# One store of all codes, loads let go as others land, and the second half's lookup regrouped, in a recommendation tower

## The reference

```python
e = jnp.stack([tbl_0[ids[:, 0]], ..., tbl_15[ids[:, 15]]], axis=1)          # (2048, 16, 16)
A = jnp.repeat(r_x0, 16, axis=1)                                            # (2048, 624, 16)
Bm = jnp.repeat(e, 39, axis=2).reshape(2048, 624, 16)
z = jnp.einsum('bnh,bnd,nk,khd,kd->bkh', A, Bm, alpha, w, hv[..., 0])
h = jnp.concatenate([z.reshape(2048, 256), dense_ctx], axis=1)
h = jnp.maximum(h @ W_top1 + b_top1, 0.0)
h = jnp.maximum(h @ W_top2 + b_top2, 0.0)
y = h @ W_top3
```

## Time and profile before

| what | value |
|---|---|
| runs | 177.66, 178.49, 180.9 us; median 178.49 us |
| profiled execution | 178.92 us, of which the profile's span is 177.0 us |
| PE busy in the span | 164.0 us (93%) |
| DVE busy | 142.5 us (80%) |
| POOL busy | 110.9 us (63%) |
| ACT busy | 66.0 us (37%) |

### The profile page before, as it was taken

The page is one execution under the profiler, slowest core; times in us unless marked ns, Lnnn a source line. Parts: engine busy times, 40 slices in busy tenths (PEclk is TensorE's granted clock), DMA queues, the critical chain, the costliest instruction groups (busy, mean ns, idle before and its releaser), DMA issues.

```text
span 177.0 us, 5041 instructions
## 1 busy us (share of the span) xinstructions
PE 164.0 (93%) x2131; PEld 124.3 (70%) x2131; DVE 142.5 (80%) x177; ACT 66.0 (37%) x176; POOL 110.9 (63%) x116
## 2 busy tenths in 40 slices
PE   6549898968997999999999999999999999999993
PEld 1338696736984879696969696969686967776671
DVE  2978797893799999999899979996999899495000
ACT  3440788084881125212431243123403341451141
POOL 2777777777747777777777777777777776000000
PEclk9999999996999999999999999999999999999999
DMA  5889999999999997989498948694559360000000
GB/s 87 307 120 327 246 275 161 270 373 264 283 334 250 345 320 150 363 248 230 79 352 240 216 160 300 189 230 104 183 219 222 48 231 6 2 4 0 0 4 0
DMA packets 15085, 34.26 MB, mean 194 GB/s; under 512 B 6618, under 2 KB 10582, under 8 KB 11990
## 3 DMA queue, kind: packets, MB, share of 16 engines
q1 hardware_dynamic: 10162, 31.51, 58.9%
q0 software_dynamic: 3584, 0.92, 6.6%
q10 hardware_dynamic: 1316, 1.50, 2.9%
HBM read 33.88 MB, written 0.04 MB: 192 GB/s over the span
## 4 chain that ended last, share of the span: by engine, by line
PE 69%; DMA 13%; DVE 4%; ACT 3%; SPq 3%; issue 3%; POOL 3%; DVEq 0%
PE bank L927 17%; PE bank L842 17%; PE bank L848 15%; PE bank L894 11%; DMA ids_half_dram<-ids_half 6%; PE bank L915 5%; PE bank L835 4%; DMA ids_b<-ids_half_dram 3%; POOL e L478 3%; DMA e<-tbl_dram,ids_all 3%; DVE prod L642 2%; SPq L446 2%; DMA ids_all<-ids_dram 1%; ACT apart L724 1%; PE bank L856 1%
## 5 line engine op out<-in xcount | busy, mean ns | idle before, releaser
L478 POOL DMA_INDIRECT e<-tbl_dram,ids_all x112 | 110.7, 988 | 38.7 <-issue 33.2
L642 DVE TENSOR_TENSOR prod<-x,bank 128x2048 f32<-128x2048 f32 x40 | 90.3, 2279 | 8.8 <-issue 4.6
L927 PE MATMUL bank<-prod,m_w 128*32 128x256 f32 x640 | 38.6, 382 | 2.5 <-DVE prod L642 2.5
L894 PE MATMUL bank<-table,onehot 125*128 125x64 bf16 (+1 forms) x288 | 31.9, 198 | 2.3 <-DVE low L537 2.3
L842 PE MATMUL bank<-tower,w_z 128*128 128x256 f32 x128 | 32.8, 403 | 0.7 <-ACT tower L743 0.7
L894 PE MATMUL bank<-low,onehot 125*128 125x64 bf16 (+1 forms) x288 | 31.8, 197 | 0.0
L894 PE MATMUL bank<-rest,onehot 125*128 125x64 bf16 (+1 forms) x288 | 31.8, 199 | 0.0
L894 PEld LDWEIGHTS bank<-table,onehot 125*128 125x128 bf16 x288 | 27.4, 98 | 5.7 <-issue 2.9
L927 PEld LDWEIGHTS bank<-prod,m_w 128*32 128x32 f32 x640 | 19.1, 109 | 17.0 <-issue 3.5
L848 PE MATMUL bank<-tower,w 128*128 128x256 f32 x128 | 30.7, 382 | 0.1
L842 PEld LDWEIGHTS bank<-tower,w_z 128*128 128x128 f32 x128 | 24.2, 199 | 6.3 <-ACT tower L743 3.1
(11 more groups left out here) (60 smaller groups left out, 85.4 us busy)
## 6 DMA issues: line engine op xcount, KB each, us to landing
x<-x_dram SPq DMA_DIRECT2D x16, 1024.0 KB, 8.1
x<-x_dram SPq DMA_DIRECT2D x16, 512.0 KB, 12.4
ids_b<-ids_half_dram SPq DMA_DIRECT2D x7, 576.0 KB
e<-tbl_dram,ids_all POOLq DMA_INDIRECT x112, 4.7
prod<-windows_c_dram ACTq DMA_DIRECT2D x1, 768.0 KB
prod<-windows_c_dram ACTq DMA_DIRECT2D x1, 512.0 KB, 5.6
w_z<-w_z_dram SPq DMA_DIRECT2D x1, 512.0 KB
w<-w_dram SPq DMA_DIRECT2D x1, 512.0 KB, 11.0
```

The source lines that it names most:

```text
L478: nc.gpsimd.indirect_dma_start(out=e[:, tile, f * D:(f + 1) * D], out_offset=None, in_=t[f"tbl_{f}"][:, :], in_offset=bass.IndirectOffsetO ...
L642: nc.vector.tensor_tensor(prod[:, s % NPROD, :].rearrange("p (q b) -> p q b", q=HP), x0[:, tile % NX, :].rearrange("p (q b) -> p q b", q=H ...
L894: made = nc.tensor.matmul(o_bank[i % 2][:, at:at + m * D], onehot[:, n % 2, g, HOT.index(f), tile * P:(tile + 1) * P], parts[part][:, KT_A ...
L927: made = nc.tensor.matmul(z_bank[q * ZW:(q + 1) * ZW, a * HB:(a + 1) * HB], m_w[:, UNIT_OF[g], hp * ZW:(hp + 1) * ZW], prod[:, s % NPROD, ...
```

## The change

- **The store.** Before, the codes of half 1 (9 rows) are stored first, and those of halves 2 to 7 in six more stores, after the loads of tiles 1 and 2. Now one store takes all 72 rows in the place of the first.
- **The loads.** Before, SPq issues all early loads without waiting for one another, except that half 2's codes wait for the six stores. Now seven waits stand among them: each such load is issued when a certain earlier load has landed. Their order is another one too.
- **Half 1's fields.** The nine fields of half 1 are divided among its three fills in another way, so that its first window piece needs two fills instead of three.
- **Half 2's planes and picks.** Plane 0 of half 2 moves on DVE from step 4 to step 2, ahead of `multiply(3)`. Its first two fills (7 and 8) move on PE from step 5 to step 4, between the contractions of steps 3 and 4; the third (9) from step 6 to step 5.
- **The windows.** On PE, `turn_windows(0, 2)` moves ahead of pick 5, `turn_windows(1, 0)` ahead of half 0's `l1`, `turn_windows(1, 1)` right behind its first part. On ACT, `spread_e(1, 0)` moves ahead of `keep_z(0)`, `spread_e(1, 1)` ahead of the emptying of `l1`, and half 3's plane 1 (line 731) one step later. On DVE the masks of fills 5 and 6 move ahead of `multiply(4)`.

```diff
+SECOND_FILLS = [[[1, 2], [4]], [[5, 12], [15]], [[7, 10, 13]]]
...
-PLANE_STEPS = {1: [0, 0], 2: [4, 4], 3: [5, 6], ...
-PICK_STEPS = {1: [BEFORE, 2, 3], 2: [5, 5, 6], 3: [9, 10, 11], ...
+PLANE_STEPS = {1: [0, 0], 2: [2, 2], 3: [5, 6], ...
+PICK_STEPS = {1: [BEFORE, 2, 3], 2: [4, 4, 5], 3: [9, 10, 11], ...
...
-    return 2 * p + 2 if n == 0 else FIRST_FILLS[n + 1]
+    return 2 * FILL_PACK[j] + 2 if n == 0 else FIRST_FILLS[1] + 2 if (n, j) == (1, 0) else FIRST_FILLS[n + 1]
...
-            sp.dma_start(ids_rows[1], ids_half[1:IDS:NH, :]).then_inc(ids_stored[0], 16)
+            sp.dma_start(ids_rows.rearrange("n f b -> f n b"), ids_half[:]).then_inc(ids_stored, 16)
...
             load_x0(1)
             load_x0(2)
-            for n in range(2, NH):
-                sp.dma_start(ids_rows[n], ids_half[n:IDS:NH, :]).then_inc(ids_stored[1], 16)
+            sp.wait_ge(in_x0[1], 16 * x0_loads(1))
+            load_ids(2)
             sp.dma_start(b_w3[:], t["b_w3"]).then_inc(in_b_w3, 16)
+            sp.wait_ge(in_x0[2], 16 * x0_loads(2))
+            load_x0(3)
+            sp.wait_ge(in_ids_b[2], 16)
             load_ctx()
             sp.dma_start(w1_z[:], ...).then_inc(in_w1, 16)
-            sp.wait_ge(ids_stored[1], 16 * (NH - 2))
-            load_ids(2)
-            load_x0(3)
+            sp.wait_ge(in_x0[3], 16 * x0_loads(3))
+            load_x0(4)
+            sp.wait_ge(in_w1, 16)
             load_ids(3)
+            sp.wait_ge(in_x0[4], 16 * x0_loads(4))
             sp.dma_start(w2[:], ...).then_inc(in_w2, 16)
-            load_x0(4)
...
                 if s == 4:
+                    spread_e(1, 0)
                     keep_z(0)
-                    spread_e(1, 0)
+                    spread_e(1, 1)
                     act.wait_ge(in_b_w3, 16)
...
                 if s == 5:
                     find_apart(3)
+                elif s == 6:
                     make_plane(3)
...
                 if s == 2:
                     for unit in CONTRACTS[2]:
                         contract(unit)
+                    turn_windows(0, 2)
                     for i in PICKS[2]:
                         pick_rows(i)
                 if s == 4:
-                    for unit in CONTRACTS[4]:
-                        contract(unit)
+                    contract(CONTRACTS[4][0])
+                    for i in PICKS[4]:
+                        pick_rows(i)
+                    contract(CONTRACTS[4][1])
+                    turn_windows(1, 0)
                     pe.wait_ge(in_ctx, 16 * N_CTX_LOADS)
                     pe.wait_ge(in_w1, 16)
                     for job in JOBS[4]:
                         fill_t(job)
+                    turn_windows(1, 1)
```

More of the change, by code:

```diff
@@ L69 @@
 HALF_FILLS = [[[4, 7, 10, 13]], [[15], [1, 2]], [[5, 12]]]
-FILLS = [(_n, _runs) for _n in range(8) for _runs in (FRONT_FILLS if _n == 0 else HALF_FILLS)]
+SECOND_FILLS = [[[1, 2], [4]], [[5, 12], [15]], [[7, 10, 13]]]
+FILLS = [(_n, _runs) for _n in range(8) for _runs in (FRONT_FILLS if _n == 0 else SECOND_FILLS if _n == 1 else HALF_FILLS)]
 FIRST_FILLS = {_n: 0 if _n == 0 else len(FRONT_FILLS) + (_n - 1) * len(HALF_FILLS) for _n in range(9)}
@@ L146 @@
 BEFORE = -1
-PLANE_STEPS = {1: [0, 0], 2: [4, 4], 3: [5, 6], **{n: [UH * (n - 1) - 4, UH * (n - 1) - 3] for n in range(4, NH)}}
-PICK_STEPS = {1: [BEFORE, 2, 3], 2: [5, 5, 6], 3: [9, 10, 11], **{n: [UH * (n - 1) - 2, UH * (n - 1) - 1, UH * (n - 1)] for n in range(4, NH)}}
+PLANE_STEPS = {1: [0, 0], 2: [2, 2], 3: [5, 6], **{n: [UH * (n - 1) - 4, UH * (n - 1) - 3] for n in range(4, NH)}}
+PICK_STEPS = {1: [BEFORE, 2, 3], 2: [4, 4, 5], 3: [9, 10, 11], **{n: [UH * (n - 1) - 2, UH * (n - 1) - 1, UH * (n - 1)] for n in range(4, NH)}}
 KEEP_STEPS = {1: [1, 4, 4], 2: [5, 6, 7], 3: [9, 10, 11], **{n: [UH * (n - 1) - 1, UH * (n - 1), UH * (n - 1) + 1] for n in range(4, NH)}}
@@ L170, in act_planes_by, with kept_at @@
     return sum(of <= n for of in ACT_HALVES)
-def kept_at(n, p):
-    return 2 * p + 2 if n == 0 else FIRST_FILLS[n + 1]
+def kept_at(n, j):
+    return 2 * FILL_PACK[j] + 2 if n == 0 else FIRST_FILLS[1] + 2 if (n, j) == (1, 0) else FIRST_FILLS[n + 1]
 PE_IDS = 1
@@ L307, in program @@
         in_small = sem("in_small")
-        ids_stored = [sem(f"ids_stored_{n}") for n in range(2)]
+        ids_stored = sem("ids_stored")
         in_ids_b = {n: sem(f"in_ids_b_{n}") for n in range(PE_IDS, NH)}
@@ L439, in _ @@
             load_x0(0)
-            sp.wait_ge(ids_stored[0], 16)
+            sp.wait_ge(ids_stored, 16)
             load_ids(1)
@@ L652, in _ @@
                     sum_rows(3)
-                for i in KEEPS.get(s, []):
+                for i in KEEPS[4] if s == 3 else KEEPS.get(s, []) if s != 4 else []:
                     mask_rows(i)
-                if s != 4:
-                    for plane in PLANES.get(s, []):
-                        make_plane(*plane)
+                for plane in PLANES.get(s, []):
+                    make_plane(*plane)
                 for i in KEEPS.get(s, []):
@@ L660, in _ @@
                 if s == 4:
-                    for plane in PLANES[4]:
-                        make_plane(*plane)
                     dve.wait_ge(in_b_w3, 16)
@@ L692, in spread_e @@
             def spread_e(n, j):
-                act.wait_ge(rows_kept, kept_at(n, FILL_PACK[j]))
+                act.wait_ge(rows_kept, kept_at(n, j))
                 for i in range(j + 1):
@@ L802, in _ @@
                     make_plane(2)
-                if g in (0, 1) and s > 0:
+                if g in (0, 1) and s not in (0, UH):
                     spread_e(n, g + 1)
@@ L998, in _ @@
                         fill_t(job)
-                if s == 1 or g == 2:
+                    turn_windows(1, 1)
+                if s == 1 or g == 2 and n > 0:
                     turn_windows(n, g)
-                elif g == 4 and n + 1 < NH:
+                elif g == 4 and 0 < n < NH - 1:
                     turn_windows(n + 1, 0)
-                fills = PICKS.get(s, []) if s > 2 else []
+                fills = PICKS.get(s, []) if s > 2 and s != 4 else []
                 units = CONTRACTS.get(s, []) if s not in (0, 2, 4) else []
@@ L1017, in _ @@
                         pick_rows(i)
[L1018 to L1022, removed]
+                if s in (UH, 2 * UH):
                     for i in fills:
```

## The result

The changed kernel was slower, by a little: 181.3 us against 179.69 for the kernel before in four runs each, ratio 1.0161 [1.0093, 1.0229]; a later set of 12 runs gave 180.33 us and 1.0069 [1.0022, 1.0115]. The second, of more runs, is the better measure. The forecast was 177.0 us with a range up to 179.6: wrong in sign. The profiled execution took 180.15 us, its span 178.3 (before 178.92 and 177.0), so the trace shows 1.3 us to be explained.

What follows compares the result with a forecast made beforehand. PE was taken to bound the kernel from step 7's contraction on, so only the start-up counted: 178.92 us profiled less 1.5 is 177.4, and runs' median 0.43 lower gives 177.0 us, range 175.0 to 179.6.

Steps and rivals of the forecast that it cites:

- 33.5 taken: Start-up: half 2's codes, behind tile 2 only, land at 33.5 us instead of 36.2, ends 32.3 and 34.5.
- 42.6 taken: Start-up: `multiply(5)` starts 9.1 us after half 2's codes land, at 42.6 us instead of 45.32, 2.7 us gained.
- The rule that step 7's contraction follows half 3's plane by 7.74 us: End of start-up: the 7.74 us from half 3's plane on DVE to step 7's contraction on PE stay as before.
- the turning point of 48.1 us: Half 3's codes: from a landing at 48.1 us on, each microsecond later is one lost.
- DVE's 8.1 us: DVE from half 2's codes: plane, two multiplications, two masks and a sum end by 33.5 + 8.1 = 41.6 us.
- Half 3's codes: 46.6 us: Start-up loads: half 3's codes land at 46.6 us, ends 44.3 and 49.8, so step 7 gains 1.5 us.
- The second rival: Start-up loads: waits leave gaps, half 3's codes land at 49.8 us, 1.7 us lost, 180.2 us; chance 0.17.
- The stores' removal returns something between nothing and the 2 us: Thin stretch of 28 to 30 us: without the six stores, half 3's codes come 1.0 us sooner.
- 40.7 us for `w_z`: Start-up loads: `w_z` lands 5.9 us or more ahead of half 3's codes, about 40.7 us; wanted at 43.
- The waits for landings cost something: Loads of tile 3, tile 4 and half 3's codes: gaps cost nothing to 3.5 us, 1.3 taken.
- The third rival: Start-up: nothing gained, `w` lands at 51.4 instead of 49.6 or the one store delays half 1's codes; 178.5 us, chance 0.13.
- What it gains there the whole gains: From step 7's contraction (55.87 us) on PE is unaltered, so its gain there is the whole kernel's gain.

Runs made afterwards that it cites:

- e1: Kernel before with one store of all codes in place of the first, without the six later stores: 179.85 us, 0.9997.
- e9: e8 with the four dense-context loads issued right behind half 2's codes instead of behind their landing: 176.74 us, 0.9872.
- e3: Changed kernel without its six waits for landings, order of the loads kept: 181.73 us, 1.0144 against the kernel before.
- e10: e8 without its five waits for landings: 181.38 us, 1.0063 against the kernel before.
- e8: Changed kernel with the dense context in whole rows, and half 3's codes and `w` ahead of tile 4: 178.0 us, 0.992 against the kernel before.
- e4: Changed kernel with half 3's plane 0 one step later on DVE, behind `multiply(6)`: 179.59 us, 1.0012 against the kernel before.
- e7: Changed kernel with half 3's codes and `w` loaded ahead of tile 4: 179.13 us, 0.9959 against the kernel before.
- e2: Changed orders on PE, DVE and ACT, with the stores and loads of the kernel before: 180.81 us, 1.0037.
- e6: Kernel before with the dense context in memory as whole rows: 179.41 us, 1.0033.
- e13: e8 with the second copy of the dense context in partitions 64 to 79 instead of 32 to 47: 176.65 us, 0.9849.
- after: The changed kernel itself, in its first profiled execution: 180.15 us.
- e11: e9 with `w_z` and `w` also laid out in whole rows of 4 KB: 177.87 us, 0.9929 against the kernel before.
- e5: Changed kernel with the dense context in memory as whole rows: 179.99 us, 0.9943 against the kernel before.
- e14: e9 with the second copy of the dense context in partitions 64 to 79: 177.29 us beside 179.44, too few runs for an interval.

## Why the prediction was wrong

**What held.** Half 2's codes landed at 30.7 us (33.5 taken; the lower end was 32.3), since tile 2, ahead of them, had landed at 29.2 us where 31.8 was counted with; whether it was the stores or the dense context's loads that had held it up no run shows. `multiply(5)` began at 41.26 us, 42.6 taken, and picks 7 and 8 stand between the contractions of steps 3 and 4. The rule that step 7's contraction follows half 3's plane by 7.74 us held at 7.77 and, in the 12 runs' profile, 7.75; so did the turning point of 48.1 us: 48.70 gives 0.6 of loss, 49.78 gives 1.66. The one store cost nothing to be seen: half 1's codes reached ACT at 21.3 us (22.6 before), and `multiply(2)`, behind half 1's fills, began at 30.00 us (30.77 before). `l1`'s clock fell as feared (0.88 in 40 to 45 us and 0.73 in 44 to 50, after PE had stood 1.84 us), and `l2` behind it waited for `w` anyway. (Two sums of the prediction are a little off without effect: the pieces of DVE's 8.1 us come to 7.7, and half of 3 × 2.29 is 3.4.)

**The step that failed** is "Half 3's codes: 46.6 us". They landed at 48.7 and 49.8 us in the two profiles. The second rival, "the steps starve the DMA engines", came true with its turning point and, at 180.2 us, nearly its price. In the first profile the price was met partly by luck: only 0.6 of the 1.3 us come by this step, the rest by PE's stand at 79 us. Two terms were mis-sized.

- *"The stores' removal returns something between nothing and the 2 us"; 1.0 was taken.* The runs show no return. e1's time can't tell 1.0 us (0.6%) from nothing, but in its trace the thin stretch is there without any of the six stores. I had read 87 GB/s as the small stores' mark; e9, where the stretch went along with the dense context's loads, shows that it belongs to them. The prediction named them ("share that stretch and stay") and still gave half of it to the stores. The change put these loads behind a wait, at 30.7 us, so the thin stretch moved to 34 to 39 us, where the kernel before moved 345 GB/s:

```profile
26.00:31.00 5.00, 4.43 (x78) 3.58 (x80) 3.91 (x9) 4.40 (x13) 3.78 (x5) 1.00 1.16 183
34.00:39.00 5.00, 3.41 (x68) 2.04 (x64) 5.00 (x4) 2.74 (x2) 3.78 (x5) 1.00 0.97 345
```

  There it delayed `w_z`, on whose landing half 3's codes now waited. I took 40.7 us for `w_z`; it was 42.9. The codes followed 5.75 us later, where the prediction had 5.9 or more: in the first profile all of the 2.1 us were lost ahead of `w_z`'s landing.

- *"The waits for landings cost something", 1.3 taken, 3.5 at most.* In 27 to 30 us the engines' share was 0.64, in 44 to 50 us 0.71: by these shares 1.1 of 3 us and up to 1.7 of 6 us stood empty, some 2.8 in place of 1.3. Only the first lies ahead of `w_z`'s landing; with the 1.0 of the stores it makes up the 2.1 us, but no run tries the two sizes one by one. In the 12 runs' profile the empty time lies elsewhere, up to 2.2 of 5 us at a share of 0.56, where tile 4 could go out only at 41.03 us, when tile 3 had landed:

```profile
39.00:44.00 5.00, 3.78 (x71) 2.93 (x69) 3.89 (x6) 1.91 (x7) 3.78 (x5) 1.00 0.56 153
```

  The Trainium skill's "DMA: Bandwidth & Descriptors", section "Anatomy of one DMA", which is headed for DMAs issued by POOL while these are issued by the sync engine, gives about 2.0 us fixed for each DMA: half 3's codes at 51.3 by all three places at full price, an estimate. The traces lie between that and the 46.6 taken, at 48.7 and 49.8. That the waits leave the engines empty does not make them a loss as a whole: without them e3 was as slow as the changed kernel and e10 slower than e8.

**The third rival too.** `w` was to be harmless up to 49.8 us and to land by 49.6. It landed at 51.5. e4's trace shows that this alone would have held PE as long. The prediction asked for the two late landings as separate cases; both hang on tile 4, behind which the change had put them, and came together. e7, which takes only this back, makes the loss go away in time, and e8 shows both landings in time.

**What the prediction did not have:** PE's stands with nothing waited for, 0.70 of the 1.3 us in the first profile. With them its premise "What it gains there the whole gains" does not hold: 0.60 us lost at step 7 became 1.3, and in e8 the 3.1 gained there became 2.0. They are the last section's.

## What to carry over

A load that waits for a landing takes over all the lateness of that landing: before the loads of a start-up are put into a chain, each link is to be priced with what shares its stretch, and the load that is wanted first must not stand behind one that is wanted later. A stretch in which full DMA engines move little belongs to some load; moving the suspected load and seeing whether the stretch goes along settles whose it is, and such a load does least harm where nothing wanted soon is queued behind it. When a wait is taken off one engine, look at the second landing that the next engine needs at the same moment, since half of a double cause gives nothing back.

## What the runs showed of the hardware

**PE stands at fixed places of its program.** With nothing waited for, PE stood inside a run of matmuls at five places, and only there. The count is that of the matmuls ahead of the place in the trace:

| count | place | stands, us |
|---|---|---|
| 469 | picks 7 and 8, behind 16 of 84 matmuls (36 to 42 us) | e3 3.65, e7 3.10, e4 0.34, e10 0.24 |
| 595 | pick 9, behind 20 of 24 (50 us) | e10 0.39 |
| 720 | a pick at 60 to 66 us, behind 41 of 48 | e10 2.11, e2 0.77, e6 0.48, e3 0.45 |
| 972 | a pick at about 79 us, behind 7 of 36 | e13 0.75, after 0.53, e7 0.29, e11 0.23, e4 0.16 |
| 1098 | `l1` at 88 us | e5 0.19 |

The places lie 126, 125, 252 and again 126 matmuls apart, each matmul with a weight load, and the one at 720 shows in e6 too, whose order on PE is that of the kernel before. The trace shows single packets of 16 KB on queues that it calls instruction; one of these queues carries 17 in a whole execution, for 2131 matmuls and as many weight loads, 251 instructions to a packet. In e3 one stands at 37.8 us, 0.8 us after the stand had begun, in e8 one at 34.0 us and no stand. The Trainium skill's "Runtime: NRT & Kernel Launch", section "Instruction fetch mechanics", says that an engine's instructions are refilled in blocks of 16 KiB, 256 of them, over its own DMA queue, and calls the cost mostly hidden. Packet and spacing agree with it (126 matmuls with their weight loads are 252 instructions, and the waits among them come on top); "hidden" does not, with stands up to 3.65 us. So a late block is what these stands look like. That it comes late because loads are queued ahead of it is a guess and not shown: e10, without any wait for a landing, stood only 0.24 us at the first place, and e7, with five, stood 3.10.

**Full DMA engines at less than half of their rate.** The four loads of the dense context, 320 KB into 16 partitions at a time, go with a stretch of 4 to 5 us in which 16 engines are full and move 122 to 169 GB/s, whether they read whole rows (e5, e8, e9) or pieces; 34 to 39 us of the kernel before moved 345. By the Trainium skill's page "SBUF — State Buffer", section "Door 1", partitions 0 to 15 and 32 to 47 lie on the same four of sixteen ports. With the second copy elsewhere the stretches of e13 and e14 moved 213 and 283 GB/s, which agrees with it; the landing of e14 agrees too, that of e13 does not.
